# Sums of squares of z: on VectorE in every batch of a graph kernel, instead of on ScalarE

## What is computed

```python
h = relu(layernorm(x));  x = x + attention(h, adj)          # 8 heads, width 16, masked softmax
h = relu(layernorm(x))
z_l, z_g, v = h @ Wl, h @ Wg, h @ Wv
A_l = zero_diag(max(cosine(z_l), 0))                         # needs |z_l| of each row
sq  = sum(z_g * z_g, axis=-1)                                # needs |z_g|^2 of each row
A_g = zero_diag(exp(-max(sq + sq.T - 2 * z_g @ z_g.T, 0) / 2))
K   = 0.9 * row_norm(A_l * causal) + 0.1 * row_norm(A_g * causal)
x   = x + (K @ v) @ Wo
```

## Time and profile before

| | before |
|---|---|
| median of three runs | 844.66 us (844.1 to 846.99) |
| the profiled execution | 843.65 us, its span 841.8 us |
| mean granted TensorE clock, share of full | 0.978 |
| busy: TensorE, VectorE, ScalarE, GpSimd | 750.9, 671.6, 588.8, 624.2 us |
| ScalarE, sums of squares (line 1264) | 60 + 60 activations of 128x128, 343 and 334 ns each, and as many reads of the accumulator, 228 and 225 ns |
| VectorE, sums of squares (line 1030) | 4 + 4 reductions of 128x128, 289 and 285 ns each |
| GpSimd, masks (line 587) | 384 of 128x512, 1298 ns each |

### The profile page before, as it was taken

How to read it: one execution, slowest core, us unless ns; L and a number is a source line. 1 busy time by engine, 2 the same in 40 slices (tenths; PEclk the granted TensorE clock), 3 DMA queues, 4 the chain that set the end, 5 groups by cost and what they waited for, 6 DMA issues and landing times.

```text
span 841.8 us, 15492 instructions
## 1 busy us (share of the span) xinstructions
PE 750.9 (89%) x4648; PEld 408.8 (49%) x4724; DVE 671.6 (80%) x1957; ACT 588.8 (70%) x1230; POOL 624.2 (74%) x707
## 2 busy tenths in 40 slices
PE   4777789899998989989898989989898999989886
PEld 3212245546464545546464544645455464636366
DVE  6777769797887979788797979788796978877266
ACT  4456786867768686876768686776868677685832
POOL 3269885978879697887869688886969688696911
PEclk9969899999999999999999999999999999999999
DMA  2312111210201121120202111020112102000000
GB/s 81 100 34 67 42 38 33 70 33 29 74 20 52 33 70 33 38 64 20 72 17 65 32 45 58 21 83 20 51 32 70 33 27 64 21 14 2 13 1 26
DMA packets 43059, 35.76 MB, mean 42 GB/s; under 512 B 6625, under 2 KB 36834, under 8 KB 42978
## 3 DMA queue, kind: packets, MB, share of 16 engines
q1 hardware_dynamic: 42978, 34.76, 13.5%
HBM read 17.70 MB, written 16.78 MB: 41 GB/s over the span
## 4 chain that ended last, share of the span: by engine, by line
PE 55%; DVE 20%; ACT 12%; issue 9%; POOL 1%; SPq 0%; DMA 0%; DVEq 0%; POOLq 0%; ACTq 0%
PE adj L761 14%; PE score L725 10%; PE pv L747 10%; DVE scrap L1021 8%; PE adj L756 7%; PE work L779 6%; ACT probs_t L1186 4%; DVE adj_cos L1039 3%; DVE rbf_arg L1048 3%; DVE adj_rbf L1053 2%; PE work L756 2%; ACT zl_square L1264 2%; PE work L895 2%; ACT z L1257 2%; ACT adj_sb L1264 1%
## 5 line engine op out<-in xcount | busy, mean ns | idle before, releaser
L587 POOL TENSOR_TENSOR probs_t<-probs_t,keep_t 128x512 int32<-128x512 int32 x384 | 488.4, 1298 | 68.6 <-ACT probs_t L1186 68.4
L1186 ACT ACTIVATE probs_t<-turned,exp_scale 128x512 f32<-128x512 f32 x512 | 344.4, 693 | 91.1 <-PE turned L733 88.1
L1021 DVE CUSTOM_DVE_ANT_0 scrap<-score,mask_add 128x512 f32<-128x512 f32 x512 | 340.0, 681 | 49.9 <-PE score L725 49.7
L725 PE MATMUL score<-qk_rows 48*128 48x512 f16 x512 | 192.2, 392 | 43.2 <-ACT probs_t L1186 23.0
L733 PE MATMUL turned<-qk_rows 50*128 50x512 f16 x512 | 191.6, 394 | 1.7 <-ACT probs_t L1186 1.1
L747 PE MATMUL pv<-probs_t,v_cols 128*32 128x512 f32 x1024 | 139.8, 619 | 1.3 <-POOL probs_t L587 1.3
L725 PEld LDWEIGHTS score<-qk_rows 48*128 48x128 f16 x512 | 44.2, 93 | 182.8 <-issue 113.2
L761 PE MATMUL adj<-v_cos,adj_cos 128*128 128x129 f32 x480 | 69.3, 286 | 0.4 <-DVE out_sb L1076 0.4
L761 PEld LDWEIGHTS adj<-v_cos,adj_cos 128*128 128x128 f32 x480 | 58.1, 190 | 21.9 <-issue 21.2
L761 PE MATMUL adj<-z,adj_rbf 128*128 128x129 f32 x480 | 64.6, 278 | 0.0
L1053 DVE SCALAR_TENSOR_TENSOR adj_rbf<-rbf_exp,mask_t 128x512 f32<-128x512 f32 x64 | 61.7, 967 | 1.0 <-ACT rbf_exp L1220 1.0
(11 more groups left out here) (170 smaller groups left out, 1094.7 us busy)
## 6 DMA issues: line engine op xcount, KB each, us to landing
q_dram<-split SPq DMA_DIRECT2D x48, 128.0 KB, 2.1
k_dram<-split SPq DMA_DIRECT2D x48, 128.0 KB, 2.1
qk_rows<-q_dram SPq DMA_DIRECT2D x64, 96.0 KB, 2.6
qk_rows<-k_dram SPq DMA_DIRECT2D x64, 96.0 KB, 2.7
x_sb<-in_x_dram SPq DMA_DIRECT2D x16, 256.0 KB, 3.2
out_dram<-out_sb SPq DMA_DIRECT2D x15, 256.0 KB, 2.5
qk_rows<-max_rows SPq DMA_DIRECT2D x128, 2.0 KB
adj_sb<-in_adj_dram SPq DMA_DIRECT2D x1, 256.0 KB, 3.1
```

The lines of the kernel that those rows point to most:

```text
L587: pool.tensor_tensor(tile, tile, keep_t[:, w // HG % T, :], ALU.mult).then_inc(probs_masked.sem, 1)
L725: pe.matmul(score_bank[u % 2][:, :], qk_rows[row:row + ROWS, b % 2, 0, h // 2, t * P:(t + 1) * P], qk_rows[row:row + ROWS, b % 2, 1, h // ...
L1021: dve.tensor_tensor_reduce(scrap[:, u % 2, :], score_bank[u % 2][:, :], mask_add[:, t, :], -1.0 / MAX_UNIT, 3.0e38, ALU.add, ALU.min, neg_ ...
L1186: act.activation(probs_t[:, kept(b, k), w % HG, :], turned_bank[w % 2][:, :], ACT.Exp, scale=exp_scale[:, 0:1]).then_inc(probs_ready.sem, 1)
```

## The change

VectorE's z_sums lose the condition that restricts them to the last batch, ScalarE's z_sums are deleted, and the table entry moves from ScalarE's group of lines to VectorE's with the same slots (71, 72, 74, 75). The last batch is as it was. Waits stay the same in kind: z_sums wait for z_copy of their tile, and tile 0 also for `floor_ready` of the batch before, now on VectorE.

```diff
-    "z_sums": (71, 72, 74, 75), "zgT_hi": (75,), "col_copy": (77,), "zlT_hi": (79,), "rbf_exp": (82, 83, 87, 89),
+    "zgT_hi": (75,), "col_copy": (77,), "zlT_hi": (79,), "rbf_exp": (82, 83, 87, 89),
...
-    "rbf_mask": (83, 84, 88, 92), "out": (93, 96, 97, 100),
+    "rbf_mask": (83, 84, 88, 92), "z_sums": (71, 72, 74, 75), "out": (93, 96, 97, 100),
...
-                if (hit := due(s, "z_sums")) and hit[0] == B - 1:
+                if hit := due(s, "z_sums"):
                     b, t = hit
                     reached(dve, z_ready, b, t + 1)
...
-                if (hit := due(s, "z_sums")) and hit[0] < B - 1:
-                    b, t = hit
-                    reached(act, z_ready, b, t + 1)
-                    if t == 0:
-                        reached(act, floor_ready, b - 1)
-                    for a in range(2):
-                        last = act.activation((zl_square, zg_square)[a][:, t, :], z[:, t, a * D:(a + 1) * D],
-                                              ACT.Square, accum_out=square_sum[:, t, a:a + 1])
-                    last.then_inc(sums_ready.sem, 1)
```

## The result

The changed kernel takes 899.44 us (median of 4, 898.84 to 903.4) against 845.47 for the kernel before (844.1 to 846.99). The ratio is 1.0648, with an interval from 1.0611 to 1.0685: 6.5% slower. The profiled execution has a span of 897.6 us where it was 841.8, which is 55.8 more. The forecast was 882 and the range 850 to 904, so the sign and the mechanism came as written, and the time came out 17 us above the forecast. In value the result is that of the hard rival (893 to 910), not that of the forecast's own case (865 to 893); it lies within the range because that reached up to most of the hard rival.

The account below looks back on a forecast made before the run. No engine alone bounds it; waits run along ScalarE, but VectorE's collisions with GpSimd's masks were taken to decide. 844.7 + 27 (batches 0 to 12) + 2 (batch 13) + 0 (batch 14) + 8 (clock) = 881.7, said 882; range 850 to 904.

Parts of the forecast that it names:

- the hard rival: GpSimd's masks win every time against VectorE's sums and the clock falls more often: 903 us (893 to 910), chance 0.22.
- the forecast's own case: VectorE's sums collide with GpSimd's masks, but VectorE goes first at tile 3's second reduction: 865 to 893 us, chance 0.53.
- lateness per batch with tile 3 won: Batches 0 to 12, VectorE ahead of the mask at tile 3: 2.1 us a batch, 27 us in all.
- tile 3 lost to the mask: GpSimd's mask goes before tile 3's second reduction: 3.3 us a batch, 43 us, instead of 2.1 and 27.
- batches 13 and 14: Batch 13's score tiles are held by reductions and masks, 2 us (0 to 4); batch 14 adds 0 (-0.5 to +1).
- clock: TensorE's clock falls after the stage in 11 batches instead of 3, 1.0 us each: +8 us (0 to +20).
- The rival without a collision: VectorE's sums keep 0.29 us under a mask: +0.15 us a batch, 846.7 us, chance 0.11.
- The replay of batch 8: Slots 71 to 76 worked through with sums and masks taking turns: q_rest 2.40 us late, the batch 2.54 late.
- The removal: Sums taken off ScalarE let zgT_hi start 0.19 us earlier at most: about 0.2 us a batch, 3 us in all.
- the first rival: The rival without a collision, under its other name: 846.7 us, no measurable change, chance 0.11.
- ScalarE as the pace: ScalarE's sums of tiles 1 to 3 set the pace, 1.7 us a batch: 819 us, or 838 to 842; chance 0.04.

Follow-up runs that it names:

- the sixth experiment: The kernel of the first experiment, but tile 0's reductions read z twice from SBUF again: 875.87 us, ratio 1.0374 to the kernel before.
- the first experiment: The changed kernel with each reduction's first operand read from z's PSUM bank in batches 0 to 14, bank freed after the sums: 839.82 us, ratio 0.9938.

## Why the prediction came out as it did

The parts of the 55.8 us between the two spans, beside the forecast's 37:

| part | forecast | measured | from |
|---|---|---|---|
| lateness per batch with tile 3 won, 13 batches | 27 (2.1 each) | 28.2 (2.17 each) | period 50.39 from batch 1 to 2, and throughout the kernel with extra matmuls; 48.22 before |
| tile 3 lost to the mask | 0 | 11.1 (10 batches at 1.11) | batch 8: tile 3's pair holds k_rest from 537.42 to 538.96, 1.54 us instead of 0.43; 12.9 by the kernel with tile 3 late |
| batches 13 and 14 | 2 | 2.0 (1.49 and 0.48) | 48.05 and 46.13 against 46.56 and 45.65 |
| clock | 8 | 14.5 (the rest, with whatever else differs) | 68 us at low clock instead of 10 |

- **That the collision decides: right.** The condition written for it was a mean above 0.5 us and durations up to 1.4. The mean of all 128 is 0.72 (the medians of the two tiles are 0.95 and 0.28), the longest 1.40. The rival without a collision is refuted by the reductions themselves, and the PSUM operand shows that the second SBUF operand is what makes them long.
- **The replay of batch 8: right to some hundredths.** Less the 32.62 of the batch's start, the score reduction of slot 72 starts at 499.45 where the replay has 499.47, q_rest at 501.16 where it has 501.16, and k at 501.95 where it has 501.96. TensorE's 1.42 and 1.37 us stood there as 1.4 each. The order of alternation between the engines, taken from two rows of adj_rbf, carried over to another instruction. adj_rbf's first value in a batch falls from 1.55 to 1.14 or so in nine of batches 1 to 12, the 0.4 that I had credited; in batches 4, 8 and 10, where the clock fell twice, it is 0.94, 0.68 and 1.10.
- **Tile 3: the step that failed first.** I had written that it hangs on 0.05 us and taken VectorE, since its request was earlier in a replay at full clock. The replay left out that the clock is low just then. I had the clock as a term of its own, 1.0 us a fall, and the tile as another. They are one: the fall makes the mask win. That gives the 11.1 us that stood only in the hard rival. Batch 0 is a case for itself: there, at full clock, the first reduction of tile 3 met a mask and took 1.18 us.
- **The clock: mis-sized.** The clock fell in 11 batches, as I had taken. But there are 14 stretches, three of these batches having two, and six of the 14 last 6.8 us where each of the three before lasts 3.4. As a whole they cost 14.5 instead of 8, if all of the rest is theirs. The "fall costs 1.0 us", read from one batch, was a price for the short one. That the clock and tile 3 together are 25 us is shown by the kernel with extra matmuls. How these 25 divide rests on the count of batches above, and is argued.
- **The removal: wrong by omission.** "At most about 0.2 us a batch" was right for the stage, and left out adj_rbf, where the earlier masks give 0.40 more. I had put just this effect in for the collision and not for the removal. In the forecast it does no harm, since it is in the 2.1. In the first rival it does: its 846.7 should have been 844.7 + 13 x (0.15 - 0.41) = 841, no loss but a gain of 0.4%. The kernel with the PSUM operand measured 839.82, its period without a fall 48.00. So the chance that I gave to a case on the other side was misplaced: the case without a collision was the case of a gain.
- **ScalarE as the pace: refuted.** The chain of waits passes through 1.7 us of ScalarE's sums a batch; without them only 0.59 comes back.

What stays open: why the low clock lasts 3.4 us in some batches and 6.8 in others, and how many of tile 0's 36 us in the sixth experiment come from the bank. That a different shape of the mask would collide less wasn't tried.

## What to carry to other kernels

Before work is moved to VectorE beside a busy GpSimd, count its SBUF operands: with two it takes turns with GpSimd's masks, whole instruction by whole instruction, and a reduction of 0.28 us becomes one of up to 1.4; with one operand still in PSUM it keeps its 0.28 to 0.29. Put it behind whatever others wait for, here k_rest, and replay the stage with the masks in it, at the clock that TensorE has at that place. Where the stage makes TensorE wait longer, the falling clock is part of the price and shifts who is first at the next collision, so the two aren't separate terms.

## What the runs showed of the hardware that wasn't expected

- A kernel with 156 extra matmuls is 25.2 us faster than the same without, since they keep the granted clock at 1.00 where it had been 0.69 and 0.66.
- A difference of 0.02 to 0.06 us in who asks first decides over 1.1 us. From batch 1 to 12 of the changed kernel GpSimd was first in all ten with a low clock there, and VectorE in both without and in all twelve of the kernel with extra matmuls.
- The kernel before had the same collision already, at adj_rbf: 1.55 and 1.16 us instead of 0.68 in most batches. Taking the sums away moved the first of the two to 1.15, and that is two thirds of what their removal gave in a batch.
- The start of a profile isn't the same each time. The kernel of the first experiment spent 34 us from 22 us on at the low clock in its profiled execution, and its times spread from 835.27 to 849.12. A few us in the first batch between two single profiles mean nothing.
